# Two attentions and three token stages of a fused transformer kernel: loads four groups ahead, shift rows by one transfer, gating moved out of the token stage, three input buffers and long rows

## The reference

```
x = x + attn0(q = layernorm(x), k = v = ctx, mask)       # 16 heads of 16, softmax, bias bo0
h = layernorm(layernorm(x)) * g1 + be1                   # the block's own norm behind an outer one
r = layernorm(x) + causal_attn1(h) @ w_o                 # 16 heads of 16
f = layernorm(r) * g2 + be2
p = softmax(f @ w_gate); top 2 of 8 experts, weights normed to 1
m = sum over the two of weight * (gelu(f @ w1[e] + b1[e]) @ w2[e] + b2[e])
x = x + m + r
x = x + attn2(q = layernorm(x), k = v = ctx)             # one head of 256, / 16 behind the softmax
x = x + (silu(x @ w_gate) * (x @ w_up)) @ w_down         # of layernorm(x), weights int / 127
```

## Time and profile before

| | us |
|---|---|
| median of three runs | 2400.95 |
| lowest, highest | 2400.32, 2408.82 |
| profiled execution, its own time | 2402.38 |
| profiled execution, span in the profile | 2400.4 |
| granted TensorE clock, mean, in parts of full speed | 0.892 |

### The profile page before, as it was taken

One profiled execution on the slowest core, in us unless ns is written; L12 is line 12 of the kernel. 1 busy time (PEld: TensorE's weight loads), 2 busy tenths in 40 slices (PEclk: granted clock), 3 DMA queues, 4 the chain that ended last, 5 costly groups with the idle time before them and its releaser, 6 DMA issues. The chain is left out here.

```text
span 2400.4 us, 40323 instructions
## 1 busy us (share of the span) xinstructions
PE 1913.7 (80%) x13306; PEld 1144.1 (48%) x13307; DVE 1491.0 (62%) x3004; ACT 1053.6 (44%) x1974; POOL 307.1 (13%) x348
## 2 busy tenths in 40 slices
PE   7846999997488269999846618999999647998997
PEld 4501222222355135555335417888888524554555
DVE  5845888884488347777458656544444356666753
ACT  3404777776133036666501116433333235554552
POOL 1000000000433000000022142111111131221000
PEclk9958999999699579999966659999999868999999
DMA  6742444420577534444166325211111321111100
GB/s 204 268 141 83 111 107 108 106 76 30 147 253 245 164 94 132 132 132 114 35 167 164 94 92 198 95 51 46 44 53 44 100 70 36 56 58 46 35 10 18
DMA packets 211807, 249.44 MB, mean 104 GB/s; under 512 B 41920, under 2 KB 163544, under 8 KB 211664
## 3 DMA queue, kind: packets, MB, share of 16 engines
q1 hardware_dynamic: 182848, 199.35, 27.5%
q10 hardware_dynamic: 22000, 29.66, 4.4%
q0 software_dynamic: 6816, 18.62, 2.8%
HBM read 155.18 MB, written 90.78 MB: 102 GB/s over the span
## 5 line engine op out<-in xcount | busy, mean ns | idle before, releaser
L803 ACT ACTIVATE a_prob<-a_psE 128x512 f32<-128x512 f32 (+3 forms) x1024 | 480.9, 521 | 375.7 <-PE a_psE L723 187.3
L699 PE MATMUL a_psS<-a_K,a_Q 97*128 97x512 bf16 (+3 forms) x1024 | 359.7, 357 | 97.1 <-DMA a_V<-s_v 32.6
L723 PE MATMUL a_psE<-a_Q,a_K 100*128 100x512 bf16 (+3 forms) x1024 | 350.1, 346 | 48.4 <-DMA a_Q<-a_nrow 26.8
L836 DVE TENSOR_REDUCE a_nm<-a_psS 128x2 f32<-128x1024 f32 x256 | 308.2, 1216 | 101.0 <-PE a_psS L699 100.4
L833 DVE TENSOR_REDUCE a_nm<-a_psS 128x1 f32<-128x128 f32 (+3 forms) x512 | 227.2, 481 | 119.0 <-PE a_psS L702 118.6
L1553 PE MATMUL ex_psY<-ex_w2h,ex_hl 128*128 x1872 | 230.4, 273 | 12.5 <-DVEq L1448 12.4
L1539 PE MATMUL ex_psH<-ex_xT,ex_w1h 128*128 128x256 f16 x1872 | 233.8, 275 | 3.4 <-ACT ex_xT L1487 2.1
L736 PE MATMUL a_psO<-a_prob,a_V 128*32 128x512 f32 (+3 forms) x2048 | 232.9, 527 | 2.0 <-ACT a_prob L803 1.4
L1497 ACT ACTIVATE ex_hf<-ex_psH,ex_b 128x256 f32<-128x256 f32 x312 | 130.7, 470 | 222.0 <-PE ex_psH L1539 217.8
L723 PEld LDWEIGHTS a_psE<-a_Q,a_K 100*128 100x128 bf16 x1024 | 100.1, 98 | 255.8 <-ACT a_prob L803 143.4
L699 PEld LDWEIGHTS a_psS<-a_K,a_Q 97*128 97x128 bf16 x1024 | 100.9, 100 | 244.8 <-DVE a_nm L833 42.2
(11 more groups left out here) (269 smaller groups left out, 2799.6 us busy)
## 6 DMA issues: line engine op xcount, KB each, us to landing
s_qk<-t_parts SPq DMA_DIRECT2D x64, 384.0 KB, 3.4
s_v<-t_vaug SPq DMA_DIRECT2D x16, 1024.0 KB, 6.4
a_V<-s_v SPq DMA_DIRECT2D x64, 256.0 KB
s_o<-a_oT SPq DMA_DIRECT2D x64, 256.0 KB, 2.2
ex_stage<-in_w SPq DMA_DIRECT2D x16, 1024.0 KB
a_K<-s_qk SPq DMA_DIRECT2D x64, 192.0 KB
a_Q<-s_qk SPq DMA_DIRECT2D x64, 192.0 KB
s_ys<-ex_yo SPq DMA_DIRECT2D x39, 256.0 KB, 2.6
```

The lines of the kernel that those rows point to most:

```text
L699: last = pe.matmul(bank[:, 0:n], Q6[s][0:K_MAX, h, t * P:(t + 1) * P], K6[s][0:K_MAX, h, 0:n], start=True, stop=not causal)
L723: last = pe.matmul(bank[:, 0:S - q0], K6[s][0:K_EXP, h, t * P:(t + 1) * P], Q6[s][0:K_EXP, h, q0:S], start=True, stop=not causal)
L803: act.activation(prob[j % NP_BUF][:, 0:n], psE[ring(G, j) % NE][:, 0:n], ACT.Exp).then_inc(p_ready, 1)
L836: dve.tensor_reduce(nm[s % NM_BUF][:, t - 1:t + 1, h], psS_all[:, (j - 1) % NS:j % NS + 1, :], axis=AX.X, op=ALU.max, negate=True).then_in ...
```

## The change

- Attentions: SP issues three loads, the shift rows of group 0, a fourth load; then in each step result(G-1), the shift rows of G+1 in one transfer, load(G+4), inverse(G-1). V lies in DRAM by batch, group of heads, partition and tile, so that a load of V is 128 rows of 2 KB.
- Token stages: xin, cin, rb and yin have three buffers, loads are issued three batches ahead; all batches are written out, no hardware loops (in la neither; ex keeps its loop). x, x1, y1 and base lie in DRAM as [batch, partition, tile, 256]: rows of 4 KB.
- t1: divide is one DVE operation of 128x1024, placed between the two splits; the bias bo is added by PE, as a product of ones with three bf16 parts of bo, whose rows DVE sets up at the start. The order of ACT's loads is cin and rb, then xin.
- t2: no gating, no b2, no gates in DRAM. The logits of all 32 tiles stay in SBUF. The divide of the next batch comes first in a batch on DVE; the norm is `half` = (xres - mean) * g, then half * rstd + b.
- ex: picks the top two from the logits of all tiles at once, computes the two weights from one exponential, and adds b2 at the output, from a 128 x 1 KB broadcast load per tile on SP; ACT does a gelu of one column early.

```diff
-def by_pairs(eng, body, peel_last=False):
-
-
-
-
-
-    for par in range(2):
-        body(par, par)
-    with eng.Fori(1, B // 2 - peel_last) as i:
-        for par in range(2):
-            body(i * 2 + par, par)
-    if peel_last:
-        for par in range(2):
-            body(B - 2 + par, par)
+def batches(body):
+
+
+
+
+
+    for n in range(B):
+        body(n, n % 2)
...
-    xin = [c.sb(f"xin{p}", [P, TT, D]) for p in range(2)]
-    cin = [c.sb(f"cin{p}", [P, DC, S]) for p in range(2)]
+    xin = [c.sb(f"xin{p}", [P, TT, D]) for p in range(NIN)]
+    cin = [c.sb(f"cin{p}", [P, DC, S]) for p in range(NIN)]
...
-            def divide(n, par):
-                for k in range(DC):
-                    pool.wait_ge(c_in[par], (n - par) * (2 * DC * 8) + 2 * DC * 16)
-                    pool.tensor_tensor(cin[par][:, k, :], cin[par][:, k, :], rb[par][:, k, :], ALU.mult
-                                       ).then_inc(div_done, 1)
-
-            def add_bias(n, par):
-                pool.wait_ge(x_in[par], (n - par) * 8 + 16)
-                pool.tensor_tensor(xin[par][:], xin[par][:], bo[:].unsqueeze(1).to_broadcast([P, TT, D]), ALU.add
-                                   ).then_inc(bias_done, 1)
...
+            def divide(n):
+                k = n % NIN
+                dve.wait_ge(c_in[k], (n // NIN + 1) * (2 * DC * 16))
+                dve.tensor_tensor(cin[k][:].rearrange("p c s -> p (c s)"), cin[k][:].rearrange("p c s -> p (c s)"),
+                                  rb[k][:].rearrange("p c s -> p (c s)"), ALU.mult).then_inc(div_done, 1)
...
+                if stage == 1 and not (isinstance(n, int) and n >= B - 2):
+                    divide(n + 2)
...
+                dve.memset(bo_rows[:], 0.0)
+                dve.memset(bo_ones[:], 1.0)
+                link(dve.tensor_copy(bo_part[0][:], bo[:]))
+                link(dve.tensor_tensor(bo_rest[:], bo[:], bo_part[0][:], ALU.subtract))
+                link(dve.tensor_copy(bo_part[1][:], bo_rest[:]))
+                dve.tensor_copy(bo_rows[0:1, :], bo_part[0][0:1, :])
+                dve.tensor_copy(bo_rows[32:33, :], bo_part[1][32:33, :])
+                dve.tensor_tensor(bo_rows[64:65, :], bo_rest[64:65, :], bo_part[1][64:65, :], ALU.subtract
+                                  ).then_inc(bias_set, 1)
+                divide(0)
+            front(0, 0, lambda: divide(1))
             link.reset()
...
-                        last = pe.matmul(psV[t][:, 0:D], cin[par][:, g, t * P:(t + 1) * P], wo[:, g, :],
-                                         start=g == 0, stop=g == DC - 1)
-                    last.then_inc(v_ps, 1)
+                        pe.matmul(psV[t][:, 0:D], cin[n % NIN][:, g, t * P:(t + 1) * P], wo[:, g, :],
+                                  start=g == 0, stop=False)
+                    pe.matmul(psV[t][:, 0:D], bo_ones[:], bo_rows[:], start=False, stop=True).then_inc(v_ps, 1)
...
+    AHEAD = 4
...
-                sp.dma_start(V[s][:], scr["v"][ds(b, 1), :, g * GH * HP:(g + 1) * GH * HP]
-                             .rearrange("o (t p) c -> p (o t) c", p=P)).then_inc(g_in[s], 16)
+                sp.dma_start(V[s][:].rearrange("p t c -> p (t c)"), scr["v"][b, g]).then_inc(g_in[s], 16)
...
-            for G in range(SLOTS // 2):
-                load(G, G)
-
-            def maxima(G, s):
+            def shift_in(G, s):
 
                 sp.wait_ge(nrow_ready, G + 1)
-                for r in range(NPART):
-                    sp.dma_start(Q6[s][KM + 1 + r:KM + 2 + r, :, :],
-                                 nrow[s % 2][r * GH:(r + 1) * GH, :]).then_inc(nrow_in[s % 2], 16)
+                sp.dma_start(Q6[s][KM + 1:KM + 1 + NPART].rearrange("r h n -> r (h n)"), nrow[s % 2][:]
+                             ).then_inc(nrow_in[s % 2], 16)
...
-            maxima(0, 0)
-            for G in range(SLOTS // 2, SLOTS):
+            for G in range(AHEAD - 1):
                 load(G, G)
+            shift_in(0, 0)
+            load(AHEAD - 1, AHEAD - 1)
 
             def step(G, s):
+                if G > 0:
+                    result(G - 1, (s - 1) % SLOTS)
                 if not last_of(G, 1):
-                    maxima(G + 1, (s + 1) % SLOTS)
-                if isinstance(G, int) and G == 0:
-                    return
-                result(G - 1, (s - 1) % SLOTS)
-                if not last_of(G, SLOTS - 1):
-                    load(G + SLOTS - 1, (s - 1) % SLOTS)
-                inverse(G - 1, (s - 1) % SLOTS)
+                    shift_in(G + 1, (s + 1) % SLOTS)
+                if not last_of(G, AHEAD):
+                    load(G + AHEAD, (s + AHEAD) % SLOTS)
+                if G > 0:
+                    inverse(G - 1, (s - 1) % SLOTS)
...
+                if not last_of(n, 1):
+                    divide(n + 1)
+                k = n % NIN
+                dve.wait_ge(x_in[k], (n // NIN + 1) * 32)
+                for t in range(TT):
+                    dve.wait_ge(v_ps, n * TT + t + 1)
+                    dve.tensor_tensor(xres[:, t, :], psV[t][:, 0:D], yin[k][:, t, :], ALU.add).then_inc(v_free, 1)
+                dve.wait_ge(v_free, n * TT + TT + TT)
                 for t in range(TT):
                     last = dve.bn_stats(stats[:, t, :], xres[:, t, :])
                 link(last)
                 for t in range(TT):
                     last = dve.bn_aggr(mv[:, t, :], stats[:, t, :])
                 last.then_inc(var_ready, 1)
+                dve.wait_ge(var_ready, n + 1)
+                for t in range(TT):
+                    last = dve.scalar_tensor_tensor(out=half[:, t, :], in0=xres[:, t, :], scalar=mv[:, t, 0:1],
+                                                    in1=lng[:], op0=ALU.subtract, op1=ALU.mult)
+                link(last)
+                if not (isinstance(n, int) and n < 2):
                     dve.wait_ge(tr_ps, n - 1)
                 dve.wait_ge(rstd_ready, n + 1)
+                for t in range(TT):
+                    last = dve.scalar_tensor_tensor(out=y[par][:, t, :], in0=half[:, t, :], scalar=rstd[:, t:t + 1],
+                                                    in1=lnb[:], op0=ALU.mult, op1=ALU.add)
+                last.then_inc(y_ready, 1)
+                dve.wait_ge(base_out[par], (n - par) * 8)
+                dve.tensor_tensor(base[par][:], xres[:], xin[k][:], ALU.add).then_inc(base_ready, 1)
+                dve.wait_ge(base_ready, n + 1)
                 dve.sem_inc(x_used, 1)
...
+            def choose(scores, best, chosen):
+                link(dve.tensor_reduce(best[:], scores[:], axis=AX.X, op=ALU.max))
+                link(dve.tensor_tensor(pos[:], scores[:], over(best[:]), ALU.is_equal))
+                link(dve.tensor_tensor(pos[:], pos[:], back[:].unsqueeze(1).to_broadcast([P, NT, E_N]), ALU.mult))
+                link(dve.tensor_reduce(topi[:], pos[:], axis=AX.X, op=ALU.max))
+                link(dve.tensor_tensor(chosen[:], pos[:], over(topi[:]), ALU.is_equal))
...
-                link(dve.tensor_tensor(scan[k][:], gate, chosen[:], ALU.mult))
-                link(dve.tensor_reduce(gsel[:, k, :], scan[k][:], axis=AX.X, op=ALU.add))
...
+            dve.wait_ge(exp_ready, 1)
+            link(dve.tensor_scalar(topi[:], top[1][:], 1.0, None, ALU.add))
+            link(dve.reciprocal(gsel[:, 0, :], topi[:]))
+            dve.tensor_tensor(gsel[:, 1, :], gsel[:, 0, :], top[1][:], ALU.mult).then_inc(slot_ready, 1)
...
-                dve.tensor_scalar(yo[q][:, 0, :], psY[0][:, 0:D], 1.0 / WSCALE, None, ALU.mult)
-                dve.tensor_scalar(yo[q][:, 1, :], psY[1][:, 0:D], 1.0 / WSCALE, None, ALU.mult)
+                dve.wait_ge(b2_in[q], (s - q) * 8 + 16)
+                for h in range(2):
+                    dve.scalar_tensor_tensor(out=yo[q][:, h, :], in0=psY[h][:, 0:D], scalar=1.0 / WSCALE,
+                                             in1=b2[q][:], op0=ALU.mult, op1=ALU.add)
...
+            act.wait_ge(gap_ready, 1)
+            act.activation(top[1][:], top[1][:], ACT.Exp).then_inc(exp_ready, 1)
+            act.activation(warm[:], warm[:], ACT.Gelu_apprx_tanh)
...
-        for n in range(2):
-            body(n, n % 2)
-        with eng.Fori(1, B // 2 - 1) as i:
-            for par in range(2):
-                body(i * 2 + par, par)
-        for n in range(B - 2, B + 1):
+        for n in range(B + 1):
             body(n, n % 2)
...
-    v0, v1 = (scratch(f"v{k}", [B, S, H * HP]) for k in range(2))
+    v0, v1 = (scratch(f"v{k}", [B, NG, P, TT * GH * HP]) for k in range(2))
...
-    x1, y1, base = (scratch(n, [B, S, D]) for n in ("x1", "y1", "base"))
+    x1, y1, base = (scratch(n, [B, P, TT, D]) for n in ("x1", "y1", "base"))
...
+    with ExitStack() as kept:
+        logits = kept.enter_context(nc.sbuf_tensor("logits", [P, NT, E_N], F32))
```

482 lines of the change are left out of this document (185 added, 297 removed).

## The result

The changed kernel takes 2256.89 us (median of four, 2250.11 to 2261.99) against 2403.64 us (four runs, 2400.32 to 2408.82) for the kernel before: the ratio is 0.9386, with a 95% interval of 0.9353 to 0.9419, so it is faster by 6%, about 147 us. The forecast was 2263. The profiled execution has a span of 2260.3 us (before: 2400.4) at a mean clock of 0.919 (before: 0.892).

The account below looks back on a forecast made before the run. Each stage was taken to have its own limit, with PE in the attentions waiting on a wrongly ordered queue. Terms -2 -25 -17 -30 -60 +1 -5 = -138 gave 2264 profiled, 2263 us median; range 2225 to 2300.

Parts of the forecast that it names:

- The terms -25 and -30: Attentions a0 and a1: SP's new order saves 25 us (20 to 28) and 30 us (22 to 32).
- what can go is the waits: Attentions: the gain is at most PE's waits for shift rows, 26.8 us in a0 and 32.3 in a1.
- The steady-state term of 0: Attentions, steady steps: loads four groups ahead still land in time, so the change is 0 us (0 to +23).
- the bound of 11.1 us: Attentions: a load has landed by 11.1 us after its first issue, within a window of 13.5 us in a1.
- load too late: Attentions rival: loads four ahead land too late, at 20 us adding 100 us in a1, 58 in a0; 2421 us; chance 0.02.
- a little late: Attentions rival: a load takes 15 us to land, a1's period becomes 10.85 us, +22 us; 2285 us; chance 0.07.
- 20.1 - 4.03 + 1.25 = 17.3: t1: batch period in us once L367's slow group is fast again and DVE gains the divide; stage saves 17 us.
- my list of limits for t2: t2, per batch: DVE about 10 us, PE 9.8 (12.7 at the lower clock), DMA 11.6.
- My 12 us a batch: t2: batch period taken as 12 us (11 to 14), part of the stage's -60.
- my start of 21 us: t2: first additions 21 us into the stage, 15 as before plus 6 for the second batch's loads.
- unrolling gives more: la rival: the loop also causes DVE's four waits of 5.9 us, which go too; 2240 us; chance 0.13.
- The DMA bound: Token stages rival: DMA limits t1 to 20 us a batch (+17) and t2 to 13 (+7); 2287 us; chance 0.17.

Follow-up runs that it names:

- eight_ahead: Changed kernel with SP's old order and depth in both attentions (shift rows behind earlier loads, loads seven ahead); 2312.32 us.
- order_alone: Kernel before with only SP's new order and loads four ahead in both attentions; 2342.96 us median, ratio 0.9733.
- three_ahead: Changed kernel with attention loads issued three groups ahead, not four; 2727.47 us.
- divide_early: Changed kernel with t1's divide of the next batch placed on DVE behind the statistics, not between the two splits; 2241.37 and 2252.0 us.
- best_loads: Changed kernel with the next batch's divide behind the statistics in t1 and t2, and t1's loads one batch earlier; 2245.27 us median, ratio 0.9334 to the kernel before.
- two_loads_first: Changed kernel with two input buffers in the token stages, and loads issued as early as two buffers allow; 2309.63 us.
- gates_late: Changed kernel with t2's divide of the next batch placed behind the statistics, not ahead of the additions; 2244.68 us.
- short_rows: Changed kernel with x, x1, y1 and base in DRAM rows of 1 KB again; 2250.0 us.
- divide_pool: Changed kernel with t1's divide back on POOL in two halves, the bias still on PE; 2252.64 us.

## Why the prediction was right

The forecast of 2263 is 6 us from the measured 2256.89, and part of that is luck: t1 gave 13 us less than its term and ex 4, and a0, a1 and t2 gave 20 more.

**Attentions, right, by the path foreseen.** The shift rows behind loads 4 to 7 were the whole of it (eight_ahead, order_alone). The terms -25 and -30 were 4 us short each. I had taken the waits for the upper end; the step that failed is that bound ("what can go is the waits"). A wait of 20 us also takes PE's clock down for what follows, and that came back as well in a0: 28.4 us before the first oT. In a1 the gain up to the first oT was 34.3, against waits of 32.3. The steady-state term of 0 held: the bound of 11.1 us for a load's time to land, worked out from one 8 KB transfer behind it, is what three_ahead gives (11.1 and 10.5). The rivals "load too late" and "a little late" fell by that number, with 2 to 3 us to spare in a1.

**t1, wrong, a quarter to 0.6 of the size.** L367 went to 1.14 us and the divide cost 1.22 us, as forecast. What failed is the step "20.1 - 4.03 + 1.25 = 17.3", which counted the busy time that DVE gains and loses and did not ask when PE gets the product. In the kernel before POOL's product is there 10.8 us before DVE's additions (668.62 to 679.39); in the changed one it is 3 us ahead of them, and a projection, which now carries the bias products, takes 4.2 us, or 5.8 with the clock down. That makes every second interval 19.5 us. The seven intervals of xo take 128.9 us, 138.9 before, so they gave 10 us where 17 were forecast. At the end of t1 the same late projection adds again: from the last batch's xo to the last store it is 35.2 us, 30.9 before and again 30.9 in divide_early. The first xo comes 1.5 us later too. divide_early puts the product early; the run best_loads, with the same divide, has the 16.95 us shown above.

**t2, -71 where -60 was forecast, with one term missing.** I read 18.2 us a batch as DVE's 15.6 us of work with short waits, and took the gating off it. For the later batches of the kernel before that reading holds:

```profile
1307.34 1.42 DVE L1023 TENSOR_TENSOR t_xres<-t_psV,t_yin 128x256 f32<-128x256 f32 x4
...
1312.01 1.38 DVE L1036 TENSOR_SCALAR t_y<-t_xres,t_mv,t_rstd 128x256 f32<-128x256 f32 x4 [1.40 <-POOL t_rstd L90]
...
1318.12 6.39 PE L1155 MATMUL t_psV<-t_wo,t_cin 128*128 128x256 f32 x16 [5.46 <-POOL t_cin L993]
```

From 1307.34 to the next additions at 1325.68 DVE waits 1.40 us for rstd, 0.44 for ACT and 0.38 with no releaser, and never for a load or for PE. But PE's projection is done at 1324.51, 1.2 us before DVE wants it, and it had waited 5.46 us for POOL's divide, which had waited for rb. So the round trip of a load through two buffers stood about 1 us behind DVE's own work, and the step that failed is that my list of limits for t2 (DVE, PE, DMA's rate) has no such term. With two buffers and all that work removed the period is 18.4 us (two_loads_first), no shorter than before. In the changed kernel the third buffer, which my list gave no price of its own, is worth 51 of the 71 us; how much of the 51 comes from the place of the divide is open, as said there. The other 20 lie behind the last addition: 42 us from there to the stage's end before, 15 in two_loads_first, less 6 us that the divide in front costs at the start. My 12 us a batch were 10.8, since DMA's rate was above the 280 GB/s I took and PE's clock at 0.73, which left DVE's 10.1 us as the nearest limit; my start of 21 us was 24.3, for the reason given there (gates_late: 16.2).

The two sums of t2's DMA: 280 GB/s at full share gave 11.6 us a batch; the Trainium skill (DMA: Bandwidth & Descriptors, section Bandwidth) with 341 GB/s gave about 9.5 (an estimate). The stage after reads 317 GB/s at full share and 10.8 us a batch, so neither was far, and the consequence drawn from the page's figure, that DMA would not be what decides, is the nearer one: short_rows lowers that rate to 301 and t2 does not move.

**ex and la.** +1 was +5 in this profile and about +1.5 over all runs; the head of the stage is 0.6 us longer when DVE starts the token tables, as ten operations of 0.42 us against the gates' load and four operations. la's -5.3 is the loop's way back. The rival "unrolling gives more" fell: the four waits outlived it and go with the gathers.

**Rivals with a chance.** The DMA bound (0.17) did not show in t2 or t1; its number for t1 was a batch of 20 us at 270 GB/s, and divide_early runs t1 at a period of 17 us.

## What to carry to other kernels

A queue that issues in order must have what an engine waits for next ahead of what will be wanted later; price it from the gap between the moment a tile is written and the moment its transfer is issued. When work moves to another engine, ask for each product when it will be there and when it is wanted, not only whose busy time changes. And before you take work off the engine that bounds a stage, look how far behind it the next limit stands: here a projection was ready only 1.2 us before it was wanted, behind a load that two buffers held back, with the DMA share at only a half. Count buffers too, not only busy times and rates.

## What the runs showed of the hardware

- Beside a POOL pair of 2.55 us, four DVE scalings that take 1.14 us alone took 3.08 (divide_pool); beside a DVE product of 1.19 us, a POOL sum of 128x4 values took 1.09 us instead of 0.20 (best_loads).
- An idle stretch of PE of 20 us was followed by work at half clock (0.50 until 210 us in a0 of the kernel before); waits of 1.5 us before the projections of t1 were followed by bias products at 0.42 us instead of 0.27 in every second batch, and by fast ones in the others.
- Rows of 4 KB instead of 1 KB moved the rate at full DMA share from 301 to 317 GB/s, and no stage's time. V's rows of 2 KB instead of 512 B moved nothing either.
- The waits of 4.5 to 6 us on DVE in la, which no record explains, go away with POOL's indirect gathers.
